# Routed additions in an AdaLN block with experts: two in flight become four, ordered by a table of token ranges

## Chip, cores and metric

One core of one Trainium2 chip runs the whole block. The metric is the device time of one execution in microseconds (us), lower is better; "before" is the median of three runs.

## What is computed

The reference takes x of 2 x 2048 tokens with 512 numbers each, and does two things to it, each behind a layer norm with a gain and a shift made from a condition vector: a gated cumulative attention with a SwiGLU product, and a mixture of experts. Only the second matters here:

```python
logits = xf @ gate_w
top_logits, top_idx = jax.lax.top_k(logits, K)          # K = 2 of E = 8 experts
top_gates = jax.nn.softmax(top_logits, axis=-1)
gates = jnp.sum(jax.nn.one_hot(top_idx, E, dtype=xf.dtype) * top_gates[..., None], axis=1)
h = gelu(jnp.einsum('nd,edh->neh', xf, w1) + b1)
out_e = jnp.einsum('neh,ehd->ned', h, w2) + b2
routed = jnp.einsum('ne,ned->nd', gates, out_e)
shared = gelu(xf @ shared_w1 + shared_b1) @ shared_w2 + shared_b2
return (routed + shared).reshape(B, S, D)
```

Each of the 4096 tokens goes to two of eight experts. Evaluated with its own inputs, the reference sends 1013, 863, 1651, 599, 915, 620, 950 and 1581 tokens to the experts 0 to 7.

## The kernel before

The engines are PE (matmul), DVE (vector), ACT (scalar), POOL (GpSimd) and SP (which issues transfers and keeps semaphores); each runs its own list of instructions in order, and the lists meet only in semaphores. The program goes through four stages: the attention part, two passes over the SwiGLU blocks ("b" and "c"), the shared expert in 8 tiles of 512 tokens ("s"), and the routed experts.

**Slots.** On the chip, every expert's tokens are written in ascending order into a list of its own in DRAM and cut into slots of 128. There are NSLOT = 71 slots; with the counts above 67 of them hold tokens (8, 7, 13, 5, 8, 5, 8 and 13 slots of the experts in turn), the last four are empty. An expert's last slot is filled up with rows behind the tokens (index 4096 and on). DVE works out in shared tile 4 which slot belongs to which expert (`slots_of_experts`, `order_of_additions`, `places`, one after each of three blocks); POOL then gathers the lists as `lblk` (71 slots by 128 rows by token and gate), PE transposes both columns in tile 5, and DVE copies them in tile 6 to `ids_t` and `gate_t` (`lists`).

**The routed stage**, slot after slot (the number of a slot is j). POOL gathers the slot's rows of h from DRAM (`gather`, L613, into one of NR = 8 buffers `rows_t`), PE transposes them (L893) and multiplies by the expert's first weights (L906, L908), ACT and DVE apply bias and gelu, PE turns the result (L920) and multiplies by the second weights (L934 to L936), ACT scales by the gate (L1253), DVE multiplies by the row gain into one of NO = 10 buffers `o_t` (L1814). POOL then adds `o_t` to the rows of `out` in DRAM, by an indirect transfer that accumulates (`scatter`, L623). On PE, slot j's turn of rows j + 3 comes first, then up j + 2, turn j + 1 and down j. On POOL, before the addition of slot j stands the gather of slot j + 11, which waits only until PE has transposed slot j + 3:

```python
            for j in range(NSLOT):
                if j + NR + AHEAD < NSLOT:
                    gather(j + NR + AHEAD)
                scatter(j)
```

**The order of the additions.** Two additions in flight that touch the same token row would lose one of the two sums. Slots of one expert never share a token; slots of two experts may. SP gives the permission: addition j starts once SP has raised `sc_go` for the j-th time. Addition j raises its own semaphore `sc_st[j % NA]` by 16 when it has landed; NA is the number in flight. For j, SP loads a number from the table `due_t` (L521), waits until the semaphore of addition j - 1 has reached it (L522), then waits for j - 2 (L525) and raises `sc_go` (L526). The number is the count that stands for addition j - 3, raised by 16 to that of j - 1 where slot j is the first of an expert ("fresh"), and never below 16.

Of the kernel before, what the change touches and what calls it, by code (L numbers as in the profile page):

```python
# [9 lines left out]
I32 = mybir.dt.int32  # L10
# [5 lines left out]
P = 128  # L16
# [18 lines left out]
def build(nc, x_tok, c, wmod, w_qkv, w_swi, w_sh, w_exp, b1s, b1r, b2p, b2s, gate_w, ident, tri, rank, tokid, ebase,  # L35
# [48 lines left out]
    with ctx:  # L84
        def at(name, kb, shape, dt=F32):
            return nc.alloc_sbuf_tensor_at(name, shape, dt, offset=BASE + int(kb * KB))
# [94 lines left out]
        ids_t = at("ids_t", 198, [P, NSLOT], U32)  # L181
        gate_t = at("gate_t", 198 + 9 / 32, [P, NSLOT])
        late_t = at("late_t", 198 + 18 / 32, [P, NSLOT])
        due_t = at("due_t", 198.875, [P, 3, NSLOT], I32)
        mean_w = sm("mean_w", [P, P])
        tri_t = sm("tri_t", [P, P])
        ident_t = sm("ident_t", [P, P])
# [35 lines left out]
        m1, m2, fst, th = [sm(n, [P, NSUB]) for n in ("m1", "m2", "fst", "th")]  # L223
        pos_f = sm("pos_f", [P, NT * NSUB, 2])
        pos = sm("pos", [P, NSUB * 2], U32)
        dues_t = at("dues_t", 27, [P, 3, NSLOT])
        jcol = sm("jcol", [P, 1])
        blk_t = sm("blk_t", [P, 1], U32)
        pay = sm("pay", [P, NSUB, 2, 2])
# [35 lines left out]
        lb_in, lb_tr, lb_ok = sem("lb_in"), sem("lb_tr"), sem("lb_ok")  # L265
        rw_in = [sem(f"rw_in{i}") for i in range(NR)]

        NA = 2
        sc_st = [sem(f"sc_st{i}") for i in range(NA)]
        settled, sc_go = sem("settled"), sem("sc_go")  # L270
        rt = sems("routed", "tr_ok xh_ok xl_ok up u1_ok u_ok gl_ok gt_ok gh_ok gl_lo dn og_ok gr_ok o_ok")
# [39 lines left out]
        def _(sp):  # L311
# [135 lines left out]
            def gates_out(u):  # L447
                sp.wait_ge(n2.gr_ok, u + 1)
                sp.dma_start(g_dram[u], gr_t[:, :]).then_inc(g_st, 16)
# [42 lines left out]
            for t in range(NT):  # L492
                if t == 1:
                    hT_out(LAST)
                if t == 5:
                    gates_out(LAST)
                if t == 3:
                    gates_out(LAST - 1)

                    sp.wait_ge(b2_ok, 1)  # L500
                    load_gain(1)
                    sp.dma_start(dues_t[:, :, :], dues.rearrange("p (k j) -> p k j", k=3)).then_inc(tb_in, 16)
                if t + 1 < NT:
                    gates_in(t + 1)
                if t + 2 < NT:
                    next_x("s", t + 2)
                if t == LAST:

                    sp.wait_ge(xl_ok, NC * NT * 3)
                    sp.dma_start(b1r_t[:, :], b1r).then_inc(b_in, 16)  # L510
                sp.wait_ge(ffn["s"].ev_ok, NSUB * (t + 1))
                sp.dma_start(tokens(out, t), r_t[:, :, :]).then_inc(out_st, 16)
                sp.wait_ge(out_st, 16 * (t + 1))
                if t < LAST:
                    load_r(x1_dram, t + 1)


            for j in range(1, NSLOT):
                for d in range(1, NA):
                    if j >= d:  # L520
                        due = sp.value_load(due_t[0:1, d - 1, j:j + 1], min_val=16, max_val=16 * NSLOT)  # L521
                        sp.wait_ge(sc_st[(j - d) % NA], due)  # L522
                        sp.sem_inc(settled)
                if j >= NA:
                    sp.wait_ge(sc_st[j % NA], 16 * (j // NA))  # L525
                sp.sem_inc(sc_go)  # L526
# [138 lines left out]
        def _(pe):  # L665
# [278 lines left out]
            def shared_tile(t):  # L944
                for s in range(NB_S + 2):
                    if s < NB_S:
                        up1(t, s)
                    if (t, s) == (LAST, NB_S + 1):

                        pe.wait_ge(ffn["s"].act_ok, NB_S * NT)  # L950
                        slot_rows(0)
                        slot_rows(1)
                    if s >= 2:
                        down("s", t, s - 2, w_shr[:, s - 2, :, :], QKV_W, NB_S)
                    if (t, s) == (0, 1):
                        logits_to_tokens(LAST - 1)
                    if (t, s) == (1, 3):
                        ranks_of(LAST - 1)
                    if (t, s) == (2, 2):
                        gates_to_rows(LAST - 1)  # L960
                    if (t, s) in ((0, 4), (0, 5), (1, 0), (1, 1)):
                        rows_to_hT(LAST, (4, 5, 0, 1).index(s))
                    if (t, s) == (1, 4):
                        logits(LAST)
                    if (t, s) == (2, 0):
                        logits_to_tokens(LAST)
                    if (t, s) == (2, 5):
                        ranks_of(LAST)
                    if (t, s) == (3, 4):
                        gates_to_rows(LAST)  # L970
                        pe.wait_ge(n2.gr_ok, LAST)
                        nc.tensor.matmul(b_x[:, 0:E], mean_w[:, :], prev[:, 0, :], start=True,
                                         stop=True).then_inc(n2.cnt_mm, 1)
                    if (t, s) == (5, 3):

                        pe.wait_ge(lb_in, 16)
                        for k in range(2):
                            ins = nc.tensor.transpose(b_x[:, k * P:k * P + NSLOT], lblk[:, :, k],
                                                      ident_t[0:NSLOT, 0:NSLOT])
                        ins.then_inc(lb_tr, 1)  # L980


# [290 lines left out]
        def _(dve):  # L1273
# [362 lines left out]
            def slots_of_experts():  # L1636

                dve.wait_ge(n2.cnt_mm, 1)
                dve.wait_ge(tb_in, 16 * 5)
                counts = b_x[:, 0:E].rearrange("p (e o) -> p e o", o=1).broadcast_to([P, E, N // P])  # L1640
                starts = thr_t[:, :].rearrange("p (o k) -> p o k", o=1).broadcast_to([P, E, N // P])
                then(nc.vector.tensor_tensor(tab_c[:, :, :], counts, starts, ALU.is_gt))
# [7 lines left out]
                then(nc.vector.tensor_tensor(tab_h[:, :, :], tab_g[:, :, :], sizes, ALU.mult))  # L1650
                then(nc.vector.reduce_sum(tab_f[:, 1, :], tab_h[:, :, :], axis=AX_X))
                then(nc.vector.tensor_tensor(tab_f[:, 1, :], jota_t[:, :], tab_f[:, 1, :], ALU.subtract))

            def order_of_additions():

                then(nc.vector.tensor_scalar(tab_f[:, 2, :], tab_f[:, 1, :], 0.0, None, ALU.is_equal))
                then(nc.vector.tensor_scalar(tab_f[:, 3, :], tab_f[:, 0, :], float(E), None, ALU.is_ge))
                then(nc.vector.tensor_tensor(tab_f[:, 2, :], tab_f[:, 2, :], tab_f[:, 3, :], ALU.is_gt))
                fresh = tab_f[:, 2:3, :].broadcast_to([P, 3, NSLOT])
                then(nc.vector.scalar_tensor_tensor(out=dues_t[:, :, :], in0=fresh, scalar=16.0, in1=dues_t[:, :, :],  # L1660
                                                    op0=ALU.mult, op1=ALU.add))
                then(nc.vector.tensor_scalar(due_t[:, :, :], dues_t[:, :, :], 16.0, None, ALU.max))

            def places():

# [17 lines left out]
            def lists():  # L1683

                dve.wait_ge(lb_tr, 1)
                nc.vector.tensor_copy(gate_t[:, :], b_x[:, P:P + NSLOT])
                nc.vector.tensor_scalar(late_t[:, :], b_x[:, 0:NSLOT], float(T_SEQ * TT), None, ALU.is_ge)
                nc.vector.tensor_copy(ids_t[:, :], b_x[:, 0:NSLOT]).then_inc(lb_ok, 1)

            def second_bias():  # L1690

# [57 lines left out]
            for t in range(NT):  # L1749
                for s in range(NB_S):  # L1750
# [15 lines left out]
                    if (t, s) == (3, 1):  # L1766
                        positions(LAST)
                        then(nc.vector.tensor_tensor(prev[:, 0, :], prev[:, 3, :], mask[:, 3, :], ALU.add))
                        gates(LAST)
                    if t == 4 and s < 3:  # L1770
                        (slots_of_experts, order_of_additions, places)[s]()
                    if (t, s) == (6, 0):
                        lists()
                if t == LAST:
                    slot_x(0)
                    slot_x(1)
# [130 lines left out]
```

## Time and profile before

| | us |
|---|---|
| median of 3 runs | 2024.28 (2022.03 to 2024.84) |
| the profiled execution, its own time | 2021.85 |
| its span, first to last instruction | 2020.0 |
| PE busy in the span | 1944.0 (96%) |
| POOL busy in the span | 434.3 (22%) |

The profile is one execution. PE's share is over all stages; the routed stage is the last 270 us, and what bounds it is read from that stretch alone. An instruction of POOL is the making of descriptors; the transfer it starts lands later and shows in the chain as a DMA piece. Times in rows are microseconds from the start of the span, except where a mean in ns is given.

### The profile page before, as it was taken

How to read it: one execution, taken by the hardware profiler on the slowest of the kernel's cores; microseconds unless marked ns; L12 is line 12 of the kernel's file. 1: busy time of each engine (PE TensorE's matmuls, PEld its weight loads, DVE VectorE, ACT ScalarE, POOL GpSimd, SP SyncE). 2: the span in 40 equal slices, each digit the busy share in tenths (PEclk: the TensorE clock that was granted, in tenths of full speed). 3: DMA queues.
4: the chain of work that ended last, by engine and by line, in shares of the span. 5: the costliest groups of instructions: out<-in, count | busy, mean ns of one | idle time of the engine just before them, and what ended most of it. 6: DMA issues, size and time to landing. Idle time of an engine off the chain costs nothing.

```text
span 2020.0 us, 26104 instructions
## 1 busy us (share of the span) xinstructions
PE 1944.0 (96%) x9104; PEld 1564.7 (77%) x9104; DVE 1281.1 (63%) x2660; ACT 645.6 (32%) x1318; POOL 434.3 (22%) x315
## 2 busy tenths in 40 slices
PE   6998999999999999999999999999999999899995
PEld 4677888888888888887887787787786667788884
DVE  6577777685545545568265456356468675588884
ACT  3545556632111111111112212212123323355552
POOL 0012000040000000026000111011061441677775
PEclk8999999999999999998999999999999999999998
DMA  5124110141101210123121321311244453578777
GB/s 225 55 89 129 52 53 27 48 141 63 37 26 63 73 62 14 51 84 135 44 84 48 101 65 53 117 65 58 91 134 170 154 176 131 177 138 146 137 140 112
DMA packets 86250, 190.07 MB, mean 94 GB/s; under 512 B 10036, under 2 KB 26804, under 8 KB 81082
## 3 DMA queue, kind: packets, MB, share of 16 engines
q1 hardware_dynamic: 63258, 131.09, 19.1%
q0 software_dynamic: 22864, 57.31, 13.5%
q8 instruction: 76, 1.25, 0.3%
q14 instruction: 52, 0.43, 0.1%
HBM read 118.67 MB, written 72.12 MB: 94 GB/s over the span
## 4 chain that ended last, share of the span: by engine, by line
PE 74%; DVE 14%; ACT 4%; issue 4%; DMA 3%; POOL 0%; DVEq 0%; POOLq 0%; SPq 0%; ACTq 0%
PE bank L667 11%; PE bank L669 11%; PE bank L668 11%; PE bank L672 8%; PE bank L674 8%; PE bank L673 8%; PE bank L906 3%; DMA out<-o_t,ids_t 2%; PE bank L833 1%; PE bank L908 1%; PE bank L686 1%; PE bank L936 1%; PE bank L934 1%; PE bank L893 1%; PE bank L935 1%
## 5 line engine op out<-in xcount | busy, mean ns | idle before, releaser
L667 PE MATMUL bank<-x_hi,w_blk 128*128 128x512 f32 x1024 | 404.3, 395 | 7.8 <-DVE x_lo L1308 5.0
L669 PE MATMUL bank<-x_hi,w_blk 128*128 128x512 f32 x1024 | 400.0, 391 | 0.0
L668 PE MATMUL bank<-x_lo,w_blk 128*128 128x512 f32 x1024 | 399.7, 390 | 0.0
L1466 DVE TENSOR_TENSOR s_t<-act_t,bank 128x512 f32<-128x512 f32 x128 | 87.8, 686 | 301.3 <-PE bank L669 295.8
L667 PEld LDWEIGHTS bank<-x_hi,w_blk 128*128 128x128 f32 x1024 | 193.0, 188 | 49.3 <-DVE x_lo L1308 6.2
L1127 ACT ACTIVATE s_hi<-s_t 128x512 fp32r<-128x512 f32 x128 | 80.9, 632 | 460.7 <-DVE s_t L1466 437.6
L669 PEld LDWEIGHTS bank<-x_hi,w_blk 128*128 128x128 f32 x1024 | 192.9, 188 | 40.8
L668 PEld LDWEIGHTS bank<-x_lo,w_blk 128*128 128x128 f32 x1024 | 193.2, 189 | 38.8
L544 POOL TENSOR_SCALAR w_blk<-raw 128x1536 fp32r<-128x1536 f32 x16 | 23.8, 1489 | 855.7 <-PE bank L674 694.1
L672 PE MATMUL bank<-w_blk,s_hi 128*128 128x512 f32 x512 | 200.6, 392 | 0.0
L674 PE MATMUL bank<-w_blk,s_lo 128*128 128x512 f32 x512 | 199.3, 389 | 0.0
L673 PE MATMUL bank<-w_blk,s_hi 128*128 128x512 f32 x512 | 199.3, 389 | 0.0
L1125 ACT ACTIVATE act_t<-bank 128x512 f32<-128x512 f32 x128 | 76.3, 596 | 354.0 <-PE bank L669 353.9
L578 POOL DMA_INDIRECT slot_list<-pay,pos x64 | 64.8, 1012 | 554.7 <-DVE pos L1602 537.3
L672 PE MATMUL bank<-w_blk,xc_hi 128*128 128x512 f32 x384 | 160.3, 417 | 16.0 <-DVE xc_lo L1356 15.7
L1469 DVE TENSOR_TENSOR s_lo<-s_t,s_hi 128x512 fp32r<-128x512 f32 x128 | 100.0, 781 | 89.5 <-ACT s_hi L1127 87.4
L674 PE MATMUL bank<-w_blk,xc_lo 128*128 128x512 f32 x384 | 152.5, 397 | 0.0
L673 PE MATMUL bank<-w_blk,xc_hi 128*128 128x512 f32 x384 | 151.7, 395 | 0.0
L623 POOL DMA_INDIRECT out<-o_t,ids_t x71 | 113.6, 1600 | 56.2 <-SPq L526 37.0
L672 PEld LDWEIGHTS bank<-w_blk,s_hi 128*128 128x128 f32 x512 | 96.1, 188 | 25.5 <-issue 6.0
L674 PEld LDWEIGHTS bank<-w_blk,s_lo 128*128 128x128 f32 x512 | 96.1, 188 | 20.1
L673 PEld LDWEIGHTS bank<-w_blk,s_hi 128*128 128x128 f32 x512 | 96.1, 188 | 19.5
(246 smaller groups left out, 3625.6 us busy)
## 6 DMA issues: line engine op xcount, KB each, us to landing
x_t<-y_scratch SPq DMA_DIRECT2D x24, 1024.0 KB
residual<-r_t SPq DMA_DIRECT2D x16, 1024.0 KB, 4.3
r_t<-residual SPq DMA_DIRECT2D x16, 1024.0 KB
raw<-w_swi POOLq DMA_DIRECT2D x12, 768.0 KB
y_scratch<-y_t SPq DMA_DIRECT2D x32, 256.0 KB, 2.7
r_t<-x_tok SPq DMA_DIRECT2D x8, 1024.0 KB
h_rows<-hrow SPq DMA_DIRECT2D x32, 256.0 KB
y_scratch<-hT SPq DMA_DIRECT2D x8, 1024.0 KB, 4.0
```

Of the source, the lines that this page charges most:

```text
L578: pool.indirect_dma_start(list_dram, bass.IndirectOffsetOnAxis(ap=pos[:, 2 * s + k:2 * s + k + 1], axis=0), pay[:, s, k, :], None).then_in ...
L623: pool.indirect_dma_start(out, bass.IndirectOffsetOnAxis(ap=ids_t[:, j:j + 1], axis=0), o_t[j % NO][:, :], None, compute_op=ALU.add).then_ ...
L667: nc.tensor.matmul(dst, w[:, 0, col:col + P], rhs_hi, start=start, stop=False)
L668: nc.tensor.matmul(dst, w[:, 0, col:col + P], rhs_lo, start=False, stop=False)
L669: return nc.tensor.matmul(dst, w[:, 1, col:col + P], rhs_hi, start=False, stop=stop)
L672: nc.tensor.matmul(dst, lhs_hi, w[:, 0, col:col + D], start=start, stop=False)
L673: nc.tensor.matmul(dst, lhs_hi, w[:, 1, col:col + D], start=False, stop=False)
L674: return nc.tensor.matmul(dst, lhs_lo, w[:, 0, col:col + D], start=False, stop=stop)
L1125: nc.scalar.activation(act_t[:, s % 2, :], bank[4 + 2 * s % 3][:, :], ACT.Silu).then_inc(f.act_ok, 1)
L1127: nc.scalar.activation(s_hi[:, s % 3, :], s_t[:, s % 2, :], ACT.Copy).then_inc(f.sh_ok, 1)
L1466: nc.vector.tensor_tensor(s_t[:, s % 2, :], act_t[:, s % 2, :], bank[4 + (2 * s + 1) % 3][:, :], ALU.mult).then_inc(f.s_ok, 1)
L1469: nc.vector.tensor_tensor(s_lo[:, s % 3, :], s_t[:, s % 2, :], s_hi[:, s % 3, :].bitcast(F32), ALU.subtract).then_inc(f.sl_ok, 1)
```

## The change

Four additions may be in flight (NA = 4). The table has three rows for slot j, for its neighbours j - 1, j - 2 and j - 3, and a row asks for the neighbour only where the two slots' ranges of tokens, from the first token to the last, meet. The first and last token of every slot come from `lblk` by two more transposes on PE, and DVE makes the table in shared tile 6 after block 1, in 19 small instructions on one partition, in place of five in tile 4 on 128 partitions. The base numbers (`dues`) are loaded in tile 5 straight into `due_t`, one partition, in place of tile 3 and 128 partitions. SP now loads and waits three times for a slot.

```diff
-        due_t = at("due_t", 198.875, [P, 3, NSLOT], I32)
+        due_t = at("due_t", 198.875, [1, 3, NSLOT], I32)
...
-        NA = 2
+        due_ok = sem("due_ok")
+        NA = 4
...
                 if t == 5:
                     gates_out(LAST)
+                    sp.dma_start(due_t[:, :, :], dues.rearrange("p (k j) -> p k j", k=3)).then_inc(tb_in, 16)
...
-                    sp.dma_start(dues_t[:, :, :], dues.rearrange("p (k j) -> p k j", k=3)).then_inc(tb_in, 16)
...
+            sp.wait_ge(due_ok, 1)
             for j in range(1, NSLOT):
                 for d in range(1, NA):
                     if j >= d:
...
+                        for k in range(2):
+                            ins = nc.tensor.transpose(b_x[0:1, (2 + k) * P:(2 + k) * P + NSLOT],
+                                                      lblk[:, k * (P - 1), 0:1], ident_t[0:NSLOT, 0:NSLOT])
                         ins.then_inc(lb_tr, 1)
...
-            def order_of_additions():
-
-                then(nc.vector.tensor_scalar(tab_f[:, 2, :], tab_f[:, 1, :], 0.0, None, ALU.is_equal))
-                then(nc.vector.tensor_scalar(tab_f[:, 3, :], tab_f[:, 0, :], float(E), None, ALU.is_ge))
-                then(nc.vector.tensor_tensor(tab_f[:, 2, :], tab_f[:, 2, :], tab_f[:, 3, :], ALU.is_gt))
-                fresh = tab_f[:, 2:3, :].broadcast_to([P, 3, NSLOT])
-                then(nc.vector.scalar_tensor_tensor(out=dues_t[:, :, :], in0=fresh, scalar=16.0, in1=dues_t[:, :, :],
-                                                    op0=ALU.mult, op1=ALU.add))
-                then(nc.vector.tensor_scalar(due_t[:, :, :], dues_t[:, :, :], 16.0, None, ALU.max))
...
+            def order_of_additions():
+
+
+                dve.wait_ge(tb_in, 16 * 5)
+                first, last = [b_x[0:1, (2 + k) * P:(2 + k) * P + NSLOT] for k in range(2)]
+                for d in range(1, NA):
+                    due, meet, meet_2 = due_t[:, d - 1, d:], meet_t[:, d:], meet_t2[:, d:]
+                    then(nc.vector.tensor_copy(meet, first[:, d:]))
+                    then(nc.vector.tensor_tensor(meet, meet, last[:, 0:NSLOT - d], ALU.is_le))
+                    then(nc.vector.tensor_copy(meet_2, first[:, 0:NSLOT - d]))
+                    then(nc.vector.tensor_tensor(meet_2, meet_2, last[:, d:], ALU.is_le))
+                    then(nc.vector.tensor_tensor(meet, meet, meet_2, ALU.mult))
+                    then(nc.vector.scalar_tensor_tensor(out=due, in0=meet, scalar=16.0, in1=due, op0=ALU.mult,
+                                                        op1=ALU.add))
+                nc.vector.tensor_scalar(due_t[:, :, :], due_t[:, :, :], 16, None, ALU.max).then_inc(due_ok, 1)
...
-                    if t == 4 and s < 3:
-                        (slots_of_experts, order_of_additions, places)[s]()
+                    if t == 4 and s < 2:
+                        (slots_of_experts, places)[s]()
                     if (t, s) == (6, 0):
                         lists()
+                    if (t, s) == (6, 1):
+                        order_of_additions()
...
-        "dues": wide(np.stack([16 * ((np.arange(slots) - d).clip(0) // 2) for d in (1, 2, 3)]).astype(np.float32)),
+        "dues": np.stack([16 * ((np.arange(slots) - d).clip(0) // 4) for d in (1, 2, 3)]).reshape(1, -1).astype(np.int32),
```

SP's list at the start of the routed stage, before: the loads for slots 1 to 4 (in brackets what SP has waited for when it comes to the instruction; `sc_st0` and `sc_st1` are raised by even and odd additions, and ISA x2 turns the loaded number into a wait value).

```order
L521 TENSOR_LOAD due_t [waits out_st]
L521 ISA x2
L521 TENSOR_LOAD due_t [waits sc_st0]
L521 ISA x2
L521 TENSOR_LOAD due_t [waits sc_st1,sc_st0]
L521 ISA x2
L521 TENSOR_LOAD due_t [waits sc_st0,sc_st1]
L521 ISA x2
```

The same place in the changed kernel: one load for slot 1, two for slot 2, three for slot 3.

```order
L524 TENSOR_LOAD due_t [waits due_ok,out_st]
L524 ISA x2
L524 TENSOR_LOAD due_t [waits sc_st0]
L524 ISA x2
L524 TENSOR_LOAD due_t [waits sc_st1]
L524 ISA x2
L524 TENSOR_LOAD due_t [waits sc_st0]
L524 ISA x2
L524 TENSOR_LOAD due_t [waits sc_st2]
L524 ISA x2
L524 TENSOR_LOAD due_t [waits sc_st1]
L524 ISA x2
```

What moved: the second load of a slot stands behind the wait for the addition just before it, and the third behind the second; from slot 3 on each slot has three loads. The wait for `due_ok` is new at the head.

DVE's list in shared tile 6, one piece of the difference, behind the second `s_lo` of the tile (`meet_t` and `meet_t_203` are the two scratch rows; the six rows come twice more, for j - 2 and j - 3).

```order
-TENSOR_TENSOR s_lo<-s_t,s_hi 128x512 x3
+TENSOR_TENSOR s_lo<-s_t,s_hi 128x512
+COPY meet_t<-bank 1x70
+TENSOR_TENSOR meet_t<-meet_t,bank 1x70
+COPY meet_t_203<-bank 1x70
+TENSOR_TENSOR meet_t_203<-meet_t_203,bank 1x70
+TENSOR_TENSOR meet_t<-meet_t,meet_t_203 1x70
+SCALAR_TENSOR_TENSOR due_t<-meet_t,due_t 1x70
...
+TENSOR_SCALAR due_t<-due_t 1x213
+TENSOR_TENSOR s_lo<-s_t,s_hi 128x512 x2
```

What moved: 19 instructions now stand between the second and the third `s_lo` of tile 6, which before followed each other.

## Rows read from the trace of the kernel before

**Rows 1.** The page: span, and busy time of each engine

```profile
span 2020.0 us, 26104 instructions
PE 1944.0 (96%) x9104; PEld 1564.7 (77%) x9104; DVE 1281.1 (63%) x2660; ACT 645.6 (32%) x1318; POOL 434.3 (22%) x315
```

**Rows 2.** Windows: busy us of each engine, clock, DMA share, GB/s

```profile
1828.00:1863.00 35.00, 35.00 (x205) 30.14 (x204) 31.27 (x62) 19.94 (x41) 28.76 (x21) 1.00 0.86 152
...
1837.53:1840.98 3.45, 3.45 (x22) 2.98 (x21) 3.07 (x7) 1.98 (x5) 2.84 (x3) 1.00 0.93 157
...
2002.19:2013.45 11.26, 0.00 (x0) 0.00 (x0) 0.00 (x0) 0.00 (x0) 6.21 (x4) 0.50 0.74 93
```

**Rows 3.** Timeline of POOL: gathers and additions, idle before and its releaser

```profile
1797.58 0.98 POOL L613 DMA_INDIRECT rows_t<-h_rows,ids_t  x1 [0.30 <-issue]
...
1913.52 1.26 POOL L613 DMA_INDIRECT rows_t<-h_rows,ids_t  x1 [0.30 <-issue]
1917.69 1.59 POOL L623 DMA_INDIRECT out<-o_t,ids_t  x1 [2.92 <-SPq L526]
1919.59 1.06 POOL L613 DMA_INDIRECT rows_t<-h_rows,ids_t  x1 [0.30 <-issue]
```

**Rows 4.** Timeline of DVE: the results of slots 41, 49 and 70

```profile
1895.95 0.69 DVE L1814 TENSOR_TENSOR o_t<-p_t,gb_row 128x512 f32<-128x512 f32 x1 [0.35 <-ACT p_t L1253]
...
1923.57 0.69 DVE L1814 TENSOR_TENSOR o_t<-p_t,gb_row 128x512 f32<-128x512 f32 x1 [0.34 <-ACT p_t L1253]
...
1998.41 0.69 DVE L1814 TENSOR_TENSOR o_t<-p_t,gb_row 128x512 f32<-128x512 f32 x1
```

**Rows 5.** Waits of the routed stage: us in total, times, longest

```profile
POOL out L623 <- SPq L526: 37.0, 19, 3.1
...
PE bank L893 <- DMA rows_t<-h_rows,ids_t: 4.9, 4, 1.6
```

**Rows 6.** Timeline of PE: the transposes of slot 53's rows

```profile
1924.36 0.66 PE L893 MATMUL bank<-ident_t,rows_t 128*128 128x128 f32 x4 [1.60 <-DMA rows_t<-h_rows,ids_t]
```

**Rows 7.** Timeline of POOL, the tail: additions 60 and 70

```profile
1985.02 1.97 POOL L623 DMA_INDIRECT out<-o_t,ids_t  x1 [1.21 <-SPq L526]
...
2013.45 1.55 POOL L623 DMA_INDIRECT out<-o_t,ids_t  x1 [1.75 <-SPq L526]
```

**Rows 8.** Timeline of POOL: additions 1, 2 and 4

```profile
1766.21 1.60 POOL L623 DMA_INDIRECT out<-o_t,ids_t  x1 [2.98 <-DVE o_t L1814]
...
1772.16 1.76 POOL L623 DMA_INDIRECT out<-o_t,ids_t  x1 [3.06 <-SPq L526]
...
1779.35 1.58 POOL L623 DMA_INDIRECT out<-o_t,ids_t  x1 [0.30 <-DVE o_t L1814]
```

**Rows 9.** Chain that ended last: start us, us, what

```profile
1935.82 0.27 SPq L521
...
1936.45 0.02 SPq L526
...
1938.45 4.18 DMA rows_t<-h_rows,ids_t
...
2007.88 4.78 DMA out<-o_t,ids_t
```

**Rows 10.** All loads of the table: ns min/median/max, first and last start

```profile
L521 SPq TENSOR_LOAD <-due_t x70: 262/270/918, 1751.1 to 2009.4; - x70
```

**Rows 11.** Timeline of DVE: small chained work in tile 4, then `s_lo` of tile 6

```profile
1647.10 0.17 DVE L1644 TENSOR_SCALAR nt_e<-nt_e 128x8 f32<-128x8 f32 x1
1647.31 0.17 DVE L1645 TENSOR_TENSOR_SCAN cum_e<-nt_e 128x8 f32<-128x8 f32 x1
...
1699.22 0.69 DVE L1734 TENSOR_TENSOR s_lo<-s_t,s_hi 128x512 fp32r<-128x512 f32 x1 [2.02 <-ACT s_hi L1141]
1704.66 0.69 DVE L1734 TENSOR_TENSOR s_lo<-s_t,s_hi 128x512 fp32r<-128x512 f32 x1 [4.75 <-ACT s_hi L1141]
```

**Rows 12.** Timeline of PE: the transposes of the lists in tile 5

```profile
1681.25 0.34 PE L978 MATMUL bank<-ident_t,lblk 71*128 71x71 f32 x2
```

More of the change, by code:

```diff
@@ L225, in build @@
         pos = sm("pos", [P, NSUB * 2], U32)
-        dues_t = at("dues_t", 27, [P, 3, NSLOT])
+        meet_t = at("meet_t", 199.71875, [1, NSLOT])
+        meet_t2 = sm("meet_t2", [1, NSLOT])
         jcol = sm("jcol", [P, 1])
@@ L1638, in slots_of_experts @@
                 dve.wait_ge(n2.cnt_mm, 1)
-                dve.wait_ge(tb_in, 16 * 5)
+                dve.wait_ge(tb_in, 16 * 4)
                 counts = b_x[:, 0:E].rearrange("p (e o) -> p e o", o=1).broadcast_to([P, E, N // P])
```

## The prediction

> **What bounds the kernel now.** The change touches little outside the routed stage, so I read the page for the span only [rows 1] and then the stage itself, in this order: windows, the timelines of POOL, DVE and PE, the waits, and the chain. Over 35 us in the middle of the stage PE is busy for all of them and the DMA engines for 0.86 of them [rows 2]: while rows arrive in time, PE sets the pace. That pace follows from two results of DVE eight slots apart: slot 41's ends at 1895.95 + 0.69 = 1896.64, slot 49's at 1924.26 [rows 4], so a slot takes 27.62 / 8 = 3.453 us. I use this as a ruler: undisturbed, the result of slot j is ready at 1896.64 + 3.453 (j - 41), for slot 4 at 1768.9 and for slot 59 at 1958.8.
>
> POOL runs behind this ruler; I call the distance from a slot's result to the start of its addition its lag. Slot 4's addition starts at 1779.35 [rows 8], lag 10.4; slot 41's at 1917.69 [rows 3], lag 21.05. It grows at the borders of experts, where an addition waits for the one just before it: in front of addition 41 POOL stood idle for 2.92 us until SP's permission [rows 3]. There are 19 such waits of 37.0 us together [rows 5]; by the slots of the experts, seven of them are the borders at 8, 15, 28, 33, 41, 46 and 54, one is slot 2, and eleven are the tail.
>
> The lag costs twice. First, a gather stands behind the late addition. Slot 53's gather starts at 1919.59, right behind addition 41, and PE stood 1.60 us for it at 1924.36 [rows 3, 6]. 1.60 us earlier it would have been in time, so PE starts to wait from a lag of 21.05 - 1.60 = 19.4. PE waits four times, 4.9 us [rows 5]. Second, when PE is done the additions that are left still have to go through. The last result is ready at 1998.41 + 0.69 = 1999.10 [rows 4], the last addition starts 14.35 us later at 2013.45 [rows 7], and from there to the end of the span are 6.55 us. From addition 60 at 1985.02 to 70 at 2013.45 they follow each other every 2.84 us, with POOL idle between them for SP [rows 7]: that is one landing time (4.78 us in the chain, [rows 9], and the way through SP and POOL) divided by two in flight.
>
> **The change, part by part.**
>
> *The border waits.* From the counts I worked out each slot's first and last token on the host: no slot's range meets that of any of the three before it (the nearest case: slot 30 ends at token 3318, before slot 27 of the expert ahead begins at 3693). Full slots of one expert are disjoint and a filled-up one begins late in the sequence while the next expert's begin early. So the table asks for nobody, and the seven border waits go. Each is about 5.95 us from addition to addition where 3.45 or less would do.
>
> *The start.* The floor of 16 in the table has a side effect. The base for j - 1 is 16 (j - 1)//4, which is 0 up to j = 4, and the floor makes it 16: additions 1, 2, 3 and 4 each wait until the one before has landed. Before, only 1 and 2 did. One such step is 1772.16 - 1766.21 = 5.95 us [rows 8]. Behind that wait the second and third load now stand. One load with its wait takes from 1935.82 to 1936.45, 0.63 us [rows 9]. So addition 2 starts at 1766.21 + 5.95 + 0.63 = 1772.8, addition 3 at + 5.95 + 1.26 = 1780.0, addition 4 at 1787.2. The gathers behind them on POOL come late with them: the lag at slot 4 is 18.3 instead of 10.4. That is 1.1 us under the 19.4 at which PE waits, so I cost it at nothing on PE; if the margin fails, each us over it is a us for PE, once. DVE's buffers give more room: ten results of 3.45 us against a lag of 18.3 and a landing of 4.8.
>
> *The lag from slot 5 to 59.* With no waits POOL goes round in a gather, an addition and twice 0.30 us. With a gather of 0.98 [rows 3] and an addition of 1.59 that is 3.17 us, and the lag shrinks by 0.28 a slot; with a gather of 1.26 [rows 3] it is 3.45 us, PE's own pace, and the lag stands still. The trace shows both: runs of seven and more slots at one lag (33 to 40, where 1913.52 is the last of the long gathers), and a short gather behind a border. I can't say from the rows which will hold. Bounds: it stays at 18.3, or it falls to 18.3 - 54 x 0.28 = 3.2. Most slots between borders kept their lag, and every border that used to shift POOL against DVE is gone, so I take a value near the upper end, 17.4. Addition 59, the last with a gather before it, then starts at 1958.8 + 17.4 = 1976.2.
>
> *PE's own stalls* (4.9 us) go, since the lag stays under 19.4. The last result then comes at 1994.2 or a little earlier, and it is not what the last addition waits for.
>
> *The tail.* Eleven steps follow from addition 59 to 70. What can set a step: POOL, 1.55 + 0.30 = 1.85 us [rows 7]; SP, three loads and waits of 0.63, 1.9 us [rows 9]; the wait for j - 4, under a half of today's 2.84; and the DMA engines. In the window of additions alone four of them started in 11.26 us at a share of 0.74 [rows 2], so one takes 11.26 x 0.74 / 4 = 2.08 us of all engines. The highest share of a slot's window was 0.93 [rows 2], by which a step is 2.24 us. Bounds are 1.9 (SP) and 2.84 (nothing gained); I take 2.25. The last addition starts at 1976.2 + 24.75 = 2000.95, against 2013.45 before: 12.5 us less.
>
> Here a rule speaks against the change. The trace has a table load at 270 ns median [rows 10]. The Trainium skill (DMA: Bandwidth & Descriptors, "Latency and other measured facts") puts the floor of such a load near 600 ns; an estimate by it is 3 x (0.60 + 0.36) = 2.9 us for SP's pass, which would be the step of the tail and leave its pace as it was. The sum goes by the row.
>
> *The rest.* On DVE 19 small instructions stand before the third `s_lo` of tile 6. Small chained ones follow each other every 0.21 us [rows 11], so 4.0 us; that `s_lo` starts at 1699.22 after 2.02 us of idling, and becomes about 2 us late. DVE idles 4.75 us before the next one, at 1704.66 [rows 11], and PE's product with the late tile comes only after that of the tile before it, so this is covered; without the cover it would be 2 us. The five wide instructions of tile 4 go, where PE does not wait either: nothing. Two transposes more on PE: two of them took 0.34 us [rows 12], and these are no larger; PE is the bound there, so + 0.1 to 0.3, I take 0.2. The table's transfer moves two tiles later and is still issued some 20 us ahead of its use; it needs one more short issue on SP and delays nothing there. The wait for `due_ok` is long satisfied when SP comes to it.
>
> *Sum.* - 12.5 + 0.2 = - 12.3 us. The profiled execution took 2021.85 us (span 2020.0); the changed one should take 2009.5, with a span near 2007.7. The median of the runs is 2.4 us above the profiled execution, so for the median 2024.28 - 12.3 = 2012.0.
>
> **Rivals.**
>
> *A. The lag melts.* POOL mostly makes the short gather, as behind the borders. Lag 3.2 to 12 at slot 59: the additions keep up, and the last one follows the last result at 1993 to 1994. At best 2013.45 - 1993.1 = 20.3 us less: 2004.0; with a lag of 12, 1970.8 + 24.75 = 1995.6, 17.9 less: 2006.4. For it: the short gather exists. Against it: the long runs at one lag.
>
> *B. The DMA engines hold the tail.* More additions in flight only queue up, each landing later, and a step stays at 2.6 to 2.84 us. The last addition is at 1976.2 + 28.6 = 2004.8 to 2007.4, 6 to 8.6 us less: 2015.7 to 2018.3. For it: the engines are at 0.74 with two in flight. Against it: windows at 0.86 and 0.93.
>
> *C. The table finds meetings,* so the change doesn't do what it says. The border waits stay, and the 7.9 us of extra lag at the start, which used to fit under 19.4, comes out as waits of PE. Addition 60 is then at 1985.02 [rows 7] + 7.9 = 1992.9 at the latest and the last ten steps of 2.25 later, at 2015.4: 2026.4 with the 0.2, and 2018.5 where addition 60 stays at 1985.02. Against it: the ranges worked out above.
>
> *D. SP becomes the bound* (slower). Three loads in SP's list for every slot, each with a wait, in place of one. If a pass takes longer than a slot, POOL waits for SP at every addition of the stage: 66 passes after addition 4 at 1787.2. It decides from (2013.45 - 1787.2) / 66 = 3.43 us a pass on. A load of 918 ns, the longest [rows 10], with the 0.36 us around it gives 3.84 us, the last addition at 2040.6, 27 us later than before: 2051.6. Against it: the median of 70 loads is 270.
>
> **How the numbers follow.** About 0.2% (4 us) is what a measurement of this kernel can tell from no change. Chances: the forecast (9 to 15 us less) 0.60, A 0.17, B 0.14, C 0.05, D 0.03, anything else 0.01. The range takes in the forecast, most of A and B: 2005 to 2018. The forecast's own range is 2009 to 2015.5. Faster by over 0.2%: forecast, A, B and a part of C, 0.94; within 0.2%: 0.03; slower: 0.03.
>
> **What would show it.** In the changed profile: additions 1 to 4 start 6 to 7.2 us apart; no border wait at 8, 15, 28, 33, 41, 46, 54; PE doesn't wait for `rows_t`; the lag after slot 4 near 18 and constant; the last eleven additions 2.25 us apart with a DMA share over 0.9, and each landing later than 4.8 us. I am wrong if the lag falls steadily (A), if the tail's step stays above 2.6 (B), if SP's waits show at the borders (C), or at every slot (D).

## The result, and the profile after

The changed kernel takes 2010.11 us (median of 4 runs, 2009.33 to 2011.13) against 2023.15 (4 runs, the three given above and one more): a ratio of 0.9935, 95% interval 0.9921 to 0.9949. The prediction was 2012.0, in a range of 2005 to 2018; 12.3 us less were forecast and 13.0 measured. The profiled execution took 2010.7 us, its span is 2008.9.

The page of the changed kernel answers to [rows 1]; PE has no more work than before, so the time came out of waiting.

```profile
span 2008.9 us, 26671 instructions
PE 1944.8 (97%) x9106; PEld 1567.2 (78%) x9106; DVE 1279.0 (64%) x2674; ACT 646.6 (32%) x1318; POOL 438.7 (22%) x315
```

The waits of the routed stage answer to [rows 5]: the view puts 37.0 us in 19 waits of POOL down to SP's permission before, now 7.5 in 6, and the wait of PE for gathered rows (4.9 us) is gone; what is left to PE from 1760 us on is one of 0.2 us.

```profile
POOL out L626 <- SPq L529: 7.5, 6, 4.3
...
PE bank L937 <- DVE gT_lo L1808: 0.2, 1, 0.2
```

POOL's timeline at the start of the stage answers to [rows 8]: additions 1 to 4 (the column behind the times is the engine), then 7. They follow each other after 6.68, 7.23 and 7.17 us, because each waits until the one before has landed. The rows of additions 1 to 3 name DVE's result as what POOL waited for, but addition 3's result had been ready for 14.4 us; those 11.0 us are waits for the permission too, and the 7.5 us of the view leave them out (as the 37.0 us leave out addition 1's 2.98 [rows 8]).

```profile
1767.89 1.59 POOL L626 DMA_INDIRECT out<-o_t,ids_t  x1 [2.94 <-DVE o_t L1829]
...
1774.57 1.57 POOL L626 DMA_INDIRECT out<-o_t,ids_t  x1 [3.79 <-DVE o_t L1829]
...
1781.80 1.58 POOL L626 DMA_INDIRECT out<-o_t,ids_t  x1 [4.25 <-DVE o_t L1829]
...
1788.97 1.58 POOL L626 DMA_INDIRECT out<-o_t,ids_t  x1 [4.30 <-SPq L529]
...
1798.57 1.59 POOL L626 DMA_INDIRECT out<-o_t,ids_t  x1 [0.30 <-DVE o_t L1829]
```

From addition 7 to addition 59 the lag behind the slot's result is 17.40 us within 0.06, at every one of the 53. No border of an expert shows. The tail, additions 59 to 70, answers to [rows 7]: from 1978.14 to 2002.28, 2.19 us a step.

```profile
1978.14 1.59 POOL L626 DMA_INDIRECT out<-o_t,ids_t  x1 [0.30 <-DVE o_t L1829]
...
1985.89 1.55 POOL L626 DMA_INDIRECT out<-o_t,ids_t  x1 [0.30 <-SPq L529]
...
1999.73 1.55 POOL L626 DMA_INDIRECT out<-o_t,ids_t  x1 [0.85 <-SPq L529]
2002.28 1.55 POOL L626 DMA_INDIRECT out<-o_t,ids_t  x1 [1.00 <-SPq L529]
```

Windows over the two halves of the tail answer to the last of [rows 2]: the DMA share was 0.74 and is 1.01 and 0.95.

```profile
1980.04:1990.10 10.06, 10.06 (x59) 8.46 (x57) 8.96 (x18) 5.58 (x12) 8.54 (x6) 1.00 1.01 132
1990.10:2002.28 12.18, 3.19 (x14) 2.00 (x12) 3.99 (x7) 2.16 (x4) 7.81 (x5) 0.77 0.95 118
```

One more number helps to compare kernels. The first result, slot 0's, ended at 1755.48 before and at 1757.19 now, 1.7 us later, and that shift arose ahead of everything the change touches in tile 4 or later: the store of shared tile 1 started at 1586.89 before and at 1588.97 now, and between 1555 and 1575 PE's granted clock was 1.00 before and 0.83 now. From slot 0's result to the end of the span are 264.5 us before and 251.7 now. I call this the stage; 12.8 us of it are gone. Each kernel has one trace, and three kernels that share the changed kernel's order of additions and nearly its lag (this one and, below, tail_no_loads and o_from_psum) have stages of 251.7, 250.9 and 250.7 us, so a difference of a us between two stages shows nothing by itself.

### The profile page after: what moved, and what is told of

Same layout as the page of the kernel before. It is cut to its first block, busy times and chain, and to the rows that moved or that the text cites. A ratio compares the mean times of both kernels' runs of the same rounds, so it can differ in the third digit from the quotient of the medians.

```text
span 2008.9 us, 26671 instructions
## 1 busy us (share of the span) xinstructions
PE 1944.8 (97%) x9106; PEld 1567.2 (78%) x9106; DVE 1279.0 (64%) x2674; ACT 646.6 (32%) x1318; POOL 438.7 (22%) x315
## 3 DMA queue, kind: packets, MB, share of 16 engines
q0 software_dynamic: 22864, 57.31, 13.8%
q8 instruction: 76, 1.25, 0.3%
## 4 chain that ended last, share of the span: by engine, by line
PE 75%; DVE 14%; issue 4%; ACT 4%; DMA 2%; SPq 0%; POOLq 0%; ACTq 0%; DVEq 0%
PE bank L670 11%; PE bank L672 11%; PE bank L671 11%; PE bank L675 8%; PE bank L677 8%; PE bank L676 8%; PE bank L909 3%; PE bank L911 2%; PE bank L896 1%; PE bank L939 1%; PE bank L937 1%; PE bank L938 1%; PE bank L836 1%; PE bank L689 1%; ACT kv_sum L1084 1%
## 5 line engine op out<-in xcount | busy, mean ns | idle before, releaser
L547 POOL TENSOR_SCALAR w_blk<-raw 128x1536 fp32r<-128x1536 f32 x16 | 23.8, 1487 | 854.3 <-PE bank L677 694.2
L675 PE MATMUL bank<-w_blk,xc_hi 128*128 128x512 f32 x384 | 160.3, 418 | 14.5 <-DVE xc_lo L1363 14.3
```

Of the source, the lines that this page charges most:

```text
L675: nc.tensor.matmul(dst, lhs_hi, w[:, 0, col:col + D], start=start, stop=False)
```

## The experiments

The theory T that I brought to them: the end is set by the lag of addition 59 plus eleven steps of the tail. The rival R: it is the four additions in flight that bring the gain. The kernel before, run beside them in three groups, took 2025.0 us (na2_table, na4_border, tail_no_loads, na4_raised), 2023.3 (na2_raised, na3_table, six_loads, o_from_psum) and 2022.9 (the last three), so each kernel is given with its ratio to the kernel before and the interval.

**Two in flight with the table** (na2_table).

```diff
-        NA = 4
+        NA = 2
...
-        "dues": np.stack([16 * ((np.arange(slots) - d).clip(0) // 4) for d in (1, 2, 3)]).reshape(1, -1).astype(np.int32),
+        "dues": np.stack([16 * ((np.arange(slots) - d).clip(0) // 2) for d in (1, 2, 3)]).reshape(1, -1).astype(np.int32),
```

> The changed kernel with two additions in flight in place of four; the table of ranges stays (its row for j - 1 alone). Theory T: the time is set by addition 59's lag behind its result and by the step of the tail. With two in flight only additions 1 and 2 wait at the start, so the lag should stand near 10.5 us in place of 17.4; the tail's step should be 2.84 us in place of 2.19. 10.5 + 11 x 2.84 = 41.7 against 17.4 + 11 x 2.19 = 41.5: the same time as the changed kernel, 2008 to 2012 us. Rival R: the gain is the tail with four in flight, and two in flight keep the slow tail at the lag of the changed kernel: 17.4 + 31.2, 7 us more, 2016 to 2018 us.

2010.09 us, ratio 0.9931 (0.9918 to 0.9945): the same as with four. Its timeline of POOL has additions 59, 60 and 70:

```profile
1970.72 1.59 POOL L626 DMA_INDIRECT out<-o_t,ids_t  x1 [0.30 <-DVE o_t L1829]
1973.44 2.04 POOL L626 DMA_INDIRECT out<-o_t,ids_t  x1 [1.12 <-SPq L529]
...
2001.63 1.55 POOL L626 DMA_INDIRECT out<-o_t,ids_t  x1 [1.23 <-SPq L529]
```

Addition 59 starts 7.4 us earlier than with four in flight (lag 10.50), the tail's step is 30.91 / 11 = 2.81 us, and they meet at the end. T holds; R falls. With two in flight, as before, the table alone brings the whole gain: its stage is 251.6 us against 264.5, of which 9.7 are the smaller lag of addition 59 (10.50 against 20.24) and 2.8 are time that PE no longer loses between slot 4's result and slot 59's.

**Four in flight without the table** (na4_border), made from the kernel before.

```diff
-        NA = 2
+        NA = 4
...
-        "dues": wide(np.stack([16 * ((np.arange(slots) - d).clip(0) // 2) for d in (1, 2, 3)]).astype(np.float32)),
+        "dues": wide(np.stack([16 * ((np.arange(slots) - d).clip(0) // 4) for d in (1, 2, 3)]).astype(np.float32)),
```

> The kernel before with four in flight; its table stays, by which the first slot of an expert waits for the additions before it. Theory T: the start costs as in the changed kernel (lag 18 at slot 4), and each of seven borders adds an addition that comes 7.2 us after the one before; each lifts the lag from 17.4 by 3.7 to above 19.4, so PE waits about 2 us at each, 14 us in all: 2020 to 2028 us, no better than before. Rival R: four in flight shorten the tail by 12 us whatever the table does, and the lag rises no further: about 2012 us.

2031.31 us, ratio 1.0039 (1.0026 to 1.0053): slower than before, beyond the upper end that T gave by 3 us. The waits of its routed stage show POOL held at the borders and PE waiting for rows eight times, 14.3 us, as T had it; the tail then takes the steps of four in flight, 23.8 us for eleven. The stage is 273.0 us, 21.3 longer than the changed kernel's.

```profile
POOL out L623 <- SPq L526: 20.0, 9, 4.4
...
PE bank L893 <- DMA rows_t<-h_rows,ids_t: 14.3, 8, 3.4
```

T reckoned with PE's 14 us alone. By the trace two things come on top. The lag stands at 26.05 in front of slot 54's addition and still at 20.51 at slot 59, 3.1 us more than in the changed kernel. And slot 59's result comes 17.4 us later after slot 4's than there, 3.1 more than PE's waits; the granted clock from 1774 to 1990 was 0.98, with PE pausing, where the changed kernel had 1.00 from 1774 to 1960. That the clock makes up those 3.1 us is likely, not shown.

**No loads in the tail** (tail_no_loads).

```diff
-                    if j >= d:
+                    if j >= d and j < 60:
```

> The changed kernel, but from slot 60 on SP neither loads from the table nor waits for the neighbours at distance 1 to 3; only the wait for j - 4 stays. No ranges meet there with these inputs, so the sums are the same. If the DMA engines set the step of the tail (as the prediction took it), the step from 66 to 70 stays at 2.4 to 2.5 us and the time at 2010 us. If SP's three loads set it, the step falls to the 2.08 us that an addition takes of the engines, and the time by 1.5 to 2 us, to 2008 to 2009 us.

2009.0 us, ratio 0.9927 (0.9914 to 0.9941), which does not stand clear of the changed kernel's. The traces tell more. In the changed kernel the first five steps of the tail are POOL's own (1.86 to 2.13 us), and the last four take 2.30 to 2.77. The chain of the changed kernel runs through SP in the last 10 us: one pass of three loads, from permission to permission, took 2.30 us, with loads of 0.27 to 0.45 us where the stage's median is 0.27.

```profile
1994.26 0.02 SPq L529
...
1994.33 0.45 SPq L524
...
1995.14 0.42 SPq L524
...
1995.93 0.27 SPq L524
...
1996.56 0.02 SPq L529
```

Without the loads POOL goes through the tail in 21.56 us in place of 24.14, each addition of the end right behind the one before:

```profile
1996.91 1.55 POOL L626 DMA_INDIRECT out<-o_t,ids_t  x1 [0.30 <-issue]
1998.78 1.55 POOL L626 DMA_INDIRECT out<-o_t,ids_t  x1 [0.30 <-issue]
```

but from its last addition to the end of the span it takes 8.22 us, not 6.62: they queue at the DMA engines, whose share is 0.99 to 1.00. From addition 59 to the end of the span are 29.8 us, against 30.8 with the loads. But o_from_psum, which has all the loads, takes 29.7 for the same stretch (22.74 and 6.93), and SP is next to nothing in its chain. So SP's loads set the pace at which POOL starts the last additions of the changed kernel, while the DMA engines, busy for 0.95 or more of the time by the windows of either kernel, set when the last one lands; that the loads cost the end anything (0.8 us by these two stages) isn't shown. Neither answer that I had set down is the whole one.

**The semaphores raised beforehand** (na4_raised): four small transfers on POOL, and every count 16 higher, so that the floor of 16 asks for nothing.

```diff
+            for k in range(NA):
+                pool.dma_start(first_t[0:1, k:k + 1], jcol_in[k:k + 1, :]).then_inc(sc_st[k], 16)
             pool.wait_ge(lb_ok, 1)
...
-                    sp.wait_ge(sc_st[j % NA], 16 * (j // NA))
+                    sp.wait_ge(sc_st[j % NA], 16 * (j // NA) + 16)
...
-                    dve.wait_ge(sc_st[(j - NO) % NA], 16 * ((j - NO) // NA + 1))
+                    dve.wait_ge(sc_st[(j - NO) % NA], 16 * ((j - NO) // NA + 2))
...
-        "dues": np.stack([16 * ((np.arange(slots) - d).clip(0) // 4) for d in (1, 2, 3)]).reshape(1, -1).astype(np.int32),
+        "dues": np.stack([16 + 16 * ((np.arange(slots) - d).clip(0) // 4) for d in (1, 2, 3)]).reshape(1, -1).astype(np.int32),
```

> The changed kernel with four small transfers on POOL ahead of the routed stage, each raising one of the four semaphores of the additions by 16, and all counts 16 higher; the floor of 16 then never asks for a landing that isn't needed, and additions 1 to 4 don't wait for the one before. Theory T: the lag at slot 4 is near 4 us, holds at 3.6, and the last addition follows the last result: 6 us less than the changed kernel, 2003 to 2005.5 us. Rival: the tail is bound by SP or the DMA engines however early it starts, since PE's results of the last four slots come 2 to 3 us apart: no more than 2 us less, 2008 us or more.

2004.08 us, ratio 0.9903 (0.9888 to 0.9919), the fastest of all: a further 6 us from mending the start (the interval lies just clear of the changed kernel's, and the stage is 245.8 us, 5.9 less). The last result and the last addition in its timelines:

```profile
1992.96 0.69 DVE L1832 TENSOR_TENSOR o_t<-p_t,gb_row 128x512 f32<-128x512 f32 x1 [0.41 <-ACT p_t L1263]
...
1994.29 1.55 POOL L627 DMA_INDIRECT out<-o_t,ids_t  x1 [0.30 <-issue]
```

The addition follows its result after 0.64 us. The lag from slot 2 to 59 is 3.58, and from slot 62 on each addition starts within 0.64 us of its result. The lag at slot 59 is 13.8 us less than in the changed kernel and the stage only 5.9, because the end now follows PE's last result.

**The same with two in flight** (na2_raised): the edit above, with NA = 2.

> The raised semaphores with two additions in flight in place of four. Theory T: what counts is the lag, and both kernels hold it at 3.6 us; only the last two additions feel the limit of two, by about 1 us: 2004 to 2006 us, within 2 us of the raised kernel with four (2004.08). Rival R: four in flight are worth their own gain once the start is mended: 4 us or more slower than with four, 2008 us or more.

2005.8 us, ratio 0.9916 (0.9902 to 0.9929), inside T's range, though the lag held at 4.62 and not at the expected 3.6. With the start mended the second pair of additions in flight makes 1.7 us by the medians and 0.5 by the stage (246.3 against 245.8), and the intervals overlap: no gain is shown.

**Three in flight with the table** (na3_table): the edit of na2_table with 3.

> The changed kernel with three in flight (rows for j - 1 and j - 2). Additions 1 to 3 wait at the start. The lag so far held at 3.58, 10.48 and 17.40 us, all a whole number of slots of 3.453 plus 0.13 us; for three in flight the start gives 14.4, so the theory that it melts down to such a value and holds there expects 13.94, and a tail step near 2.2 us: addition 59 3.5 us earlier than with four, 2005.5 to 2008.5 us. If the holding values are an accident of those kernels, the lag ends elsewhere. If time didn't depend on the lag it would be 2010 us like two and four.

2006.53 us, ratio 0.9916 (0.9903 to 0.993). The lag held at 13.94 (13.67 at slots 21 and 53) from slot 3 to 59, as expected; the stage is 248.0 us, 3.7 less than with four. Its tail takes 2.09 us a step, so the fourth addition in flight gains nothing there and costs one more wait at the start. The two intervals overlap by 0.0009, so the times alone don't quite part three from four.

**Each number loaded twice** (six_loads).

```diff
-                        due = sp.value_load(due_t[0:1, d - 1, j:j + 1], min_val=16, max_val=16 * NSLOT)
-                        sp.wait_ge(sc_st[(j - d) % NA], due)
-                        sp.sem_inc(settled)
+                        for _ in range(2):
+                            due = sp.value_load(due_t[0:1, d - 1, j:j + 1], min_val=16, max_val=16 * NSLOT)
+                            sp.wait_ge(sc_st[(j - d) % NA], due)
+                            sp.sem_inc(settled)
```

> The changed kernel with each table number loaded and waited for twice, six passes a slot in place of three (rival D of the prediction made real). A pass of 0.63 us makes 3.8 us, over PE's 3.453: the additions of the whole stage should come 3.8 to 3.9 us apart and the last at 1789 + 66 x 3.85 = 2043, PE waiting for its rows: 2046 to 2056 us. If SP's passes overlap with its waits, so that they were never near the pace, the time stays below 2015 us.

2095.29 us, ratio 1.0356 (1.0338 to 1.0373), far above the expected 2046 to 2056: the mechanism is real and its price larger than I wrote. POOL's additions come 4.45 us apart, each behind SP:

```profile
1896.84 1.59 POOL L627 DMA_INDIRECT out<-o_t,ids_t  x1 [1.58 <-SPq L530]
...
1901.29 1.59 POOL L627 DMA_INDIRECT out<-o_t,ids_t  x1 [1.07 <-SPq L530]
```

A turn of six passes of 0.62 us would be 3.7; the chain has one long load in nearly every turn, mostly of 0.8 to 0.96 us.

```profile
1903.04 0.27 SPq L525
...
1903.66 0.91 SPq L525
...
1904.99 0.26 SPq L525
```

Why one load in six takes 0.9 us isn't settled; in the changed kernel the longest is 1.03, and a turn of three passes (1.9 us, or 2.6 with the longest) has room for it inside 3.45 us.

**Why the lag holds.** In four kernels the values at which it held were 3.58, 10.48, 13.94 and 17.40 us: each 0.12 to 0.14 over a whole number of slots of 3.453 us. Something that repeats with the slots catches POOL. The first try (o_from_psum) took ACT's copy out, and with it one of the two SBUF inputs of DVE's result:

```diff
-                dve.wait_ge(rt.og_ok, j + 1)
+                dve.wait_ge(rt.dn, j + 1)
...
-                nc.vector.tensor_tensor(o_t[j % NO][:, :], p_t[j % 2][:, :], gb_row[:, :],
-                                        ALU.mult).then_inc(rt.o_ok, 1)
+                nc.vector.scalar_tensor_tensor(out=o_t[j % NO][:, :], in0=bank_o[j % 2][:, :],
+                                               scalar=gate_t[:, j:j + 1], in1=gb_row[:, :],
+                                               op0=ALU.mult, op1=ALU.mult).then_inc(rt.o_ok, 1)
```

> The changed kernel, but DVE makes the result of a slot straight from PSUM (bank x gate x row gain in one instruction), without ACT's copy p_t; the instruction then has one input in SBUF in place of two. It asks why the lag holds. Theory L: POOL's gather is stretched from 0.98 to 1.26 us while it meets that instruction of DVE, and without the meeting the lag shrinks by 0.28 us a slot to under 5 us (rival A): 2002 to 2006 us. Rival M: another instruction of DVE, or something else, sets the holding places, and the lag holds somewhere above 10 us: 2007 to 2012 us.

2009.41 us, ratio 0.9932 (0.9918 to 0.9945), and the lag held at 17.65: rival M. Then I laid the timelines of DVE and POOL beside each other. First the changed kernel in a held stretch:

```profile
1851.90 0.75 DVE L1819 SCALAR_TENSOR_TENSOR gb_row<-gbd_t,late_t,gbs_t 128x512 f32<-128x512 f32 x1
...
1852.26 1.26 POOL L616 DMA_INDIRECT rows_t<-h_rows,ids_t  x1 [0.30 <-SPq L529]
```

and na2_raised, whose lag held at 4.62, off the series:

```profile
1853.26 0.69 DVE L1832 TENSOR_TENSOR o_t<-p_t,gb_row 128x512 f32<-128x512 f32 x1 [0.35 <-ACT p_t L1263]
...
1853.56 1.25 POOL L617 DMA_INDIRECT rows_t<-h_rows,ids_t  x1 [0.30 <-SPq L530]
```

The gather starts 0.39 us before gb_row ends (1852.65) in the one and 0.39 us before o_t ends (1853.95) in the other. Both DVE instructions read two operands from SBUF. From 1790 us on, 52 of the changed kernel's gathers took over 1.1 us, and every one of them starts 0.4 us before the end of a gb_row. Two kernels tested that, both made from o_from_psum: no_gb_row leaves the gain's instruction out (the second sequence gets the first one's gain),

```diff
-                nc.vector.scalar_tensor_tensor(out=gb_row[:, :], in0=gbd_t[:, :], scalar=late_t[:, j:j + 1],
-                                               in1=gbs_t[0][:, :], op0=ALU.mult, op1=ALU.add).then_inc(rt.gr_ok, 1)
-                dve.wait_ge(rt.gr_ok, j + 1)
                 dve.wait_ge(rt.dn, j + 1)
...
-                                               scalar=gate_t[:, j:j + 1], in1=gb_row[:, :],
+                                               scalar=gate_t[:, j:j + 1], in1=gbs_t[0][:, :],
```

> As o_from_psum, and DVE's instruction for the row gain (gb_row, two inputs in SBUF) is left out as well; the result takes the first sequence's gain for all rows, so the second sequence is scaled wrongly. In every held lag so far the gather starts 0.39 us before the end of a DVE instruction with two inputs in SBUF (gb_row in the changed kernel and o_from_psum, o_t in na2_raised and in slots 33 to 40 of the kernel before). Theory P: the gather is held until that instruction ends; with none of them left the gather takes 0.98 us everywhere, the lag falls by 0.27 us a slot to under 5 us, and the time is 2002 to 2005 us. Rival: the coincidence is one of phase; the lag holds above 10 us: 2007 us or more.

and gb_row_psum keeps it with one input in PSUM, so that its numbers are not the gain.

```diff
+                dve.wait_ge(rt.dn, j + 1)
-                nc.vector.scalar_tensor_tensor(out=gb_row[:, :], in0=gbd_t[:, :], scalar=late_t[:, j:j + 1],
+                nc.vector.scalar_tensor_tensor(out=gb_row[:, :], in0=bank_o[j % 2][:, :], scalar=late_t[:, j:j + 1],
                                                in1=gbs_t[0][:, :], op0=ALU.mult, op1=ALU.add).then_inc(rt.gr_ok, 1)
```

> Control for no_gb_row: DVE keeps both instructions, with the same shapes, but the gain's instruction reads the bank in PSUM in place of one SBUF input, so its numbers are not the gain and the output is wrong. DVE has as much to do as in o_from_psum, only with one SBUF input each. Theory P expects short gathers and a lag that falls to under 5 us here too: 2002 to 2006 us. If it is DVE's amount of work that holds the lag, it holds near 17.6 as in o_from_psum: 2008 to 2011 us.

2005.2 us, ratio 0.9915 (0.99 to 0.993), and 2005.8 us, ratio 0.9918 (0.9903 to 0.9933): the first 0.2 us above the range of theory P, the second inside it. Their intervals overlap that of o_from_psum, so the times alone decide nothing; the traces do. The view of all gathers (ns min/median/max), first in the changed kernel, where 54 of 71 took over 1.1 us:

```profile
L616 POOL DMA_INDIRECT rows_t<-h_rows,ids_t x71: 952/1247/1492, 1730.0 to 1976.6; - x71
```

then in no_gb_row, where none is (gb_row_psum: 952/990/1047):

```profile
L616 POOL DMA_INDIRECT rows_t<-h_rows,ids_t x71: 949/987/1044, 1729.9 to 1962.7; - x71
```

In no_gb_row the lag falls from 17.91 at slot 5 to 3.59 at slot 59, 0.27 us a slot, and is gone at slot 62. That is rival A of the prediction, made to happen. In the control DVE is busy for 147.4 of the 160 us from 1790 on (150.7 in o_from_psum, 142.3 in the changed kernel), and no gather is stretched and the lag falls from 15.26 at slot 4 to 1.18 at slot 59; so it isn't DVE's load. The gathers of both kernels pass through every phase of DVE's period on the way, so it isn't one place in time either. The trace thus bears out, in its direction, a rule of the Trainium skill (SBUF — State Buffer, "Who interferes with whom"): a DVE instruction with two SBUF inputs contends with a GpSimd instruction that reads SBUF. The price here is 0.26 us on a gather of 0.99.

**Both mendings that leave the result whole** (raised_psum): na4_raised with the edit of o_from_psum.

> The two changes that leave the result whole, together: the raised semaphores and the result made from PSUM. The lag should be near 4 us as in na4_raised and the last results 0.3 us or so earlier for want of ACT's copy: 2003 to 2004.5 us, against 2004.08 for na4_raised. The rival, that the longer DVE instruction (0.75 against 0.69 us) costs the pace of a slot, expects 2005 us or more.

2006.54 us, ratio 0.992 (0.9904 to 0.9936): not faster than na4_raised, though the intervals overlap. The expectation missed. The lag held at 0.38, which is o_from_psum's 17.65 less five slots, but the stage is 247.0 us against 245.8. Near its start PE stands still once, which it does not in na4_raised:

```profile
1768.64 0.49 PE L912 MATMUL bank<-w_all,xT_hi 128*128 x1 [1.14 <-issue]
```

The last result then comes 0.6 us later after slot 0's than in na4_raised, and the end of the span 0.6 us later after the last result. What held PE isn't settled, and with one trace of each kernel neither is whether the 1.2 us are a cost of the edit. The pace of a slot stayed at 3.45 us, so the rival's reason isn't borne out, though its range was hit.

## Why the prediction was right

**The border waits** went, all seven, as worked out from the ranges. Their worth was not in themselves but in the lag they no longer pile up: na2_table against the kernel before shows it, 9.7 us at slot 59.

**The start** was right to 0.15 us: steps of 6.58, 7.21 and 7.21 us were forecast, 6.68, 7.23 and 7.17 measured, the lag at slot 4 18.15 (forecast 18.3). That PE would not wait was right too.

**The lag** was taken at 17.4 and was 17.40. The prediction said itself that the rows couldn't tell which gather would hold, and its bounds went from 3.2 to 18.3. That the value fits to 0.01 us is luck; the choice between the bounds was a good guess rather than a reading: the held stretches in the trace of before pointed to it, but the value came from no rule, and the cause (a gather caught by DVE) was only found afterwards.

**The tail** was right in size, 2.25 us a step against 2.19, but by a mean of two paces that the prediction did not have: the first five steps are POOL's own, 1.86 to 2.13 us, and the last four come behind SP at 2.30 to 2.77. Right was that the DMA engines are full and bound the end. The bound from SP was too low: three passes were put at 1.9 us, and took 2.30 at the end, with loads of up to 0.45 us in that pass. The pass of 2.9 us that the prediction estimated from the Trainium skill (DMA: Bandwidth & Descriptors, "Latency and other measured facts") was too dark: the page has a load near 600 ns, the median of the 207 here is 273 ns.

**The rest.** Counted from slot 0's result, the last addition was forecast at 245.5 us and came at 245.1. The span is 2008.9 and not 2007.7, because slot 0's result came 1.7 us later. DVE's 19 instructions came 0.25 us apart, not 0.21, 4.7 us in all. The `s_lo` behind them started at 1703.48, and the next still had 2.18 us of idling before it:

```profile
1698.78 0.21 DVE L1694 COPY meet_t<-bank 1x70 f32<-1x70 f32 x1
...
1703.29 0.26 DVE L1701 TENSOR_SCALAR due_t<-due_t 1x213 int32<-1x213 int32 x1
1703.48 0.67 DVE L1747 TENSOR_TENSOR s_lo<-s_t,s_hi 128x512 fp32r<-128x512 f32 x1
1706.33 0.69 DVE L1747 TENSOR_TENSOR s_lo<-s_t,s_hi 128x512 fp32r<-128x512 f32 x1 [2.18 <-ACT s_hi L1148]
```

The store of tile 6 starts 1.68 us after that of the kernel before (1720.58 and 1718.90), as the store of tile 5 did (1696.31 and 1694.64): it cost nothing, as said.

**What the sum hid.** It put 12.5 us on the way from the start to the last addition, and did not split them. Four in flight shorten the tail by 11 x (2.81 - 2.19) = 6.8 us, and the two further waits at the start, which the floor makes of four in flight, lengthen the lag by 17.40 - 10.50 = 6.9 us. The sum had both terms and the prediction did not say that they cancel; na2_table shows it. Rival C was the right one to fear: without the table four in flight lose (1.0039), and na4_border took 2031 where rival C, which has the same border waits, had 2018.5 to 2026.4.

## What to carry to other kernels

When a queue of work drains behind the bounding engine, ask for the lag at which it runs and what sets it, before making the drain faster: here a mended start was worth 6 us, and for twice as many transfers in flight no gain was shown. A floor under a wait value (16 here) asks for a landing where none is needed, and so makes each of the additions 1 to NA wait for the one before; raising the semaphores beforehand did away with it. Where two engines repeat with one period, a small collision can hold them at a fixed distance, as here from slot 7 to 59, so that a lag once made doesn't melt.

## What I had not expected of the hardware

A gather's descriptor instruction on POOL grew from 0.99 to 1.25 us when it started 0.39 us before the end of a DVE instruction with two SBUF inputs, and this phase held for more than 50 slots. A table load of SP took 0.26 to 0.27 us mostly, but 0.4 to 0.96 in a part of cases (one in nearly each turn of six passes), so that six passes took 4.45 us in place of 3.7. With the tail's additions back to back (tail_no_loads) the DMA engines were busy for 0.99 to 1.00 of the time at 127 to 129 GB/s.
